# Attention and MLP block on one core: another unit order, with column-tiled products in three runs a unit instead of four

## What is computed

```python
tp = (silu(time_emb) @ Wt + bt)[:, None, :]          # six modulation vectors
h = layernorm(x, g1, be1) * (1 + scale_msa) + shift_msa
q, k, v = split(h @ Wqkv + bqkv)                     # 16 heads of 32
attn = softmax(einsum('blhd,bmhd->bhlm', q, k) * scale)
x = x + gate_msa * (einsum('bhlm,bmhd->blhd', attn, v) @ Wproj + bproj)
h = layernorm(x, g2, be2) * (1 + scale_mlp) + shift_mlp
x = x + gate_mlp * (gelu(h @ W1 + b1) @ W2 + b2)
# then RMSNorm, scale and shift with quantized conditioning weights
```

## Time and profile before

| | us |
|---|---|
| median of 3 runs | 3763.23 (3762.49 to 3764.1) |
| the profiled execution | 3764.97 |
| its span, first to last instruction | 3763.0 |

### The profile page before, as it was taken

How to read it: one execution, slowest core, us unless ns; L and a number is a source line. 1 busy time by engine, 2 the same in 40 slices (tenths; PEclk the granted TensorE clock), 3 DMA queues, 4 the chain that set the end, 5 groups by cost and what they waited for, 6 DMA issues and landing times.

```text
span 3763.0 us, 49948 instructions
## 1 busy us (share of the span) xinstructions
PE 3715.0 (99%) x18430; PEld 2646.7 (70%) x18430; DVE 2453.7 (65%) x4107; ACT 1821.0 (48%) x3276; POOL 1940.8 (52%) x631
## 2 busy tenths in 40 slices
PE   8899999999999999999999999999999999999998
PEld 6688885555555565656565656888888888888887
DVE  5577668888888888888888883333343443443443
ACT  3222225666666666666666665333333333333333
POOL 1000005999999999999999996322222322222221
PEclk9999999999999999999999999999999999999999
DMA  8677876667776777677767755111111111111110
GB/s 286 231 237 241 254 251 142 147 143 160 169 159 148 162 168 157 150 160 170 159 148 161 170 129 159 45 40 50 45 60 45 37 45 37 45 37 45 37 45 23
DMA packets 219003, 479.38 MB, mean 127 GB/s; under 512 B 22809, under 2 KB 61721, under 8 KB 202633
## 3 DMA queue, kind: packets, MB, share of 16 engines
q1 hardware_dynamic: 200616, 344.08, 32.4%
q0 software_dynamic: 18144, 132.13, 17.1%
HBM read 225.36 MB, written 117.60 MB: 91 GB/s over the span
## 4 chain that ended last, share of the span: by engine, by line
PE 89%; POOL 4%; issue 2%; DVE 2%; DMA 2%; ACT 1%; SPq 0%; POOLq 0%; DVEq 0%; ACTq 0%
PE psum L718 12%; PE psum L1276 11%; PE psum L1290 11%; PE psum L581 10%; PE psum L583 10%; PE psum L582 10%; PE psum L1952 6%; PE psum L1948 6%; PE psum L1950 6%; PE psum L1321 4%; POOL probs_round L1555 4%; PE psum L1304 2%; PE psum L1901 1%; DMA token_stats<-packed 0%; DVE qk_out L1155 0%
## 5 line engine op out<-in xcount | busy, mean ns | idle before, releaser
L1100 DVE TENSOR_REDUCE max_part<-psum 128x1 f32<-128x512 f32 x2048 | 1272.7, 679 | 73.4 <-PE psum L718 72.0
L1555 POOL TENSOR_TENSOR probs_round<-probs_round,probs_round 128x2048 f32<-128x2048 f32 x189 | 884.8, 4682 | 126.3 <-PE psum L1290 109.2
L2117 DVE TENSOR_TENSOR g_parts<-g_full,g_parts 128x512 fp32r<-128x512 f32 x256 | 262.7, 1026 | 802.3 <-ACT g_parts L2006 802.3
L1276 PE MATMUL psum<-q_stack,k_stack 98*128 98x512 f32 x2048 | 774.8, 404 | 0.7 <-ACT probs L1422 0.5
L718 PE MATMUL psum<-k_stack,q_stack 96*128 96x512 f32 x2048 | 763.1, 403 | 0.5
L1422 ACT ACTIVATE probs_round<-psum 128x512 f32<-128x512 f32 x1024 | 542.3, 601 | 337.5 <-PE psum L1276 331.6
L1422 ACT ACTIVATE probs<-psum 128x512 f32<-128x512 f32 x1024 | 546.1, 605 | 225.1 <-PE psum L1276 209.0
L1555 POOL TENSOR_TENSOR probs_round<-probs_round,probs 128x2048 f32<-128x2048 f32 x124 | 570.1, 4598 | 9.7
L2002 ACT ACTIVATE g_full<-psum,cols 128x512 f32<-128x512 f32 x256 | 176.6, 690 | 802.2 <-PE psum L583 801.8
L718 PEld LDWEIGHTS psum<-k_stack,q_stack 96*128 96x128 f32 x2048 | 387.0, 189 | 191.5 <-DVE max_part L1100 113.8
L2213 POOL TENSOR_TENSOR y_out<-y_out,rows 128x512 f32<-128x512 f32 x60 | 77.2, 1286 | 857.3 <-DVE y_out L2152 857.3
(11 more groups left out here) (189 smaller groups left out, 4949.8 us busy)
## 6 DMA issues: line engine op xcount, KB each, us to landing
probs<-probs POOLq DMA_DIRECT2D x126, 1024.0 KB, 7.7
qk_parts<-qk_out SPq DMA_DIRECT2D x128, 512.0 KB, 4.6
k_stack<-qk_parts SPq DMA_DIRECT2D x96, 512.0 KB, 6.8
q_stack<-qk_parts SPq DMA_DIRECT2D x192, 256.0 KB, 5.5
v_rows<-v_out SPq DMA_DIRECT2D x64, 256.0 KB, 4.3
v_group<-v_rows SPq DMA_DIRECT2D x32, 512.0 KB, 9.9
gated_attention<-gated SPq DMA_DIRECT2D x64, 256.0 KB, 4.5
x<-in_x SPq DMA_DIRECT2D x16, 1024.0 KB, 9.4
```

The costliest lines, as they stand in the source:

```text
L1100: dve.reduce_max(max_part[:, n:n + 1], psum[:, TURNS[at.turn][0], :], AX.X).then_inc(dve_smax, 1)
L1276: pe.matmul(psum[:, ST[n % 3], :], k_stack[G % 2][0:ROWS, h, kt * P:(kt + 1) * P], q_stack[u % 3][0:ROWS, h, :], start=True, stop=True).th ...
L1555: pool.tensor_tensor(total[:, :, :], total[:, :, :], probs(u, kt)[:, :, :], ALU.add).then_inc(pool_sum, 1)
```

## The change

Two strings are replaced, and one condition in `pool_add`. The counts of all letters stay as they are.

```diff
-    ORDER = ("sgsmmmssmsmaVlVsmsswmmsmsmmVVmsmssmmsmmsmssVV!s"
-             "msmsmsmsmstrmspDVVmjmsjjjnmsmsjsmsjjsmsmjsmjjjj")
+    ORDER = ("gsmssmmsmwVVmsmmsmssmmalVVs!smsjmssmmsjmsmjssmj"
+             "smsmsjsmmsmsjsmsmjsmjmVVDtVrVpnsmsjmmjsmssmjsmj")
...
-    POOL_ORDER = "-1-3-6A-7B5"
+    POOL_ORDER = "-3A-6-7B15"
...
         def pool_add(pool, u, kt):
             total = probs(u, KT - ROTATING)
-            first = kt == SUMS[0]
+            first = kt == (LAST_SUMS if u == NU - 2 else SUMS)[0]
```

## The result

| | before | after |
|---|---|---|
| median, us | 3762.86 (4 runs) | 3943.93 (3939.74 to 3946.5, 4 runs) |
| span of the profiled execution, us | 3763.0 | 3942.3 |
| mean granted clock of PE | 0.997 | 0.977 |

The ratio is 1.048, with a 95% interval of 1.0469 to 1.0495: slower by 181 us. The forecast was slower by 106 us, 3869.2, with a range that ended at 3924. The direction and the wait were as forecast, the cost of the wait was not.

A forecast was written before the change was run, and what follows sets the result against it. PE was taken as the bound in full units, POOL's chain of sums in early ones. Terms -17.3 + 3 + 6.5 - 1.8 + 106.6 + 9 gave +106 us, a median of 3869.2 us, range 3850 to 3924.

The forecast's parts named there:

- The load term's wait: At the first maximum behind "!" in even units, PE waits 4.1 us for keys and queries; bounds 3.75 and 5.9.
- The load term's price: In 26 even full units each wait costs its 4.1 us: +106.6 us, bounds 97 and 153.
- The early units: Units 2, 4, 6, 8, where POOL's chain bounds: the late load costs 2.2 us each, +9 us.
- One run fewer: Column-tiled runs per unit fall from four to three: -0.33 us in each of 52 full units, -17.3 us.
- "!" among ordinary products: The maxima's transpose, moved from a run's end, costs 0.06 us in 52 units: +3 us, upper bound +12.
- Start and tail: Stage 1's extra maxima delay POOL's first sum, +6.5 us; fewer maxima in unit 62 shorten the tail, -1.8 us.
- POOL's order: GpSimd's reordered sums: the chain from V of tile 4 to D stays as long, 0 us.
- The loads in time: Rival: last part lands within 9.1 us of issue, both load terms vanish; -9.6 us, 3753.6 us; chance 0.05.
- The overlap in full: Rival: GpSimd's DMAs B and A share bandwidth equally with the load, landing 16 us, stall 7 us; 3956 us; chance 0.08.
- DVE as the bound: Rival: DVE's idle time runs out, the 26 odd full units grow 1.2 us; +31, 3900 us; chance 0.08.
- the long run: In VVDVV DVE gets no maximum for some 4.6 us of PE time; its slack covers this, costed at nothing.
- D waiting for POOL inside the run: Rival: D waits inside the long run and the saved 0.33 us returns; +17, 3886 us; chance 0.03.

The follow-up runs named there:

- the kernel with five runs: The kernel before, with its first run of two column-tiled groups split by moving one score between them: 3778.61 us, ratio 1.0044.
- the kernel with cut loads: The changed kernel with key and query loads cut in two by heads, each half with its own semaphore: 3755.39 us, ratio 0.9982 to the kernel before.
- the new sums alone: The kernel before with GpSimd's new order of sums and its changed condition, unit order left as it was: 3983.51 us, ratio 1.059.

## Why the prediction was right and wrong

The sum of the differences, from D's starts: 26 even full units of 33.06 instead of 26.84 us, +162; 26 odd ones, -5.5; the four early even units 32.05 in the mean instead of 26.67 (26.25, and 1.7 us more in the first of them, see below), +21.5; the first D +4.1; the last unit and tail -2.5. Together +179, the difference of the spans.

- **The load term's wait: right, its length partly by luck.** A wait at the first maximum behind "!", 30 times, never in odd units. Its length was forecast as 4.1 us, with bounds 3.75 and 5.9, and measured as 4.10 in the mean of PE's idle times. The forecast added 0.35 us for overlaps to a landing of 12.85 us from two samples. That landing was read short: rows 5 give one number for two issues, and in the first sample the last part went out at 1493.41, not 1493.2, and landed 13.2 us behind the first issue. So its slack was 2.3 us and not 2.7. The mean of all 30 loads before is 13.2, and after it is 13.4: the new place cost some 0.2, and A nothing that the runs can tell. The place of the first maximum was right, 9.3 us behind the issue instead of 9.1.
- **The load term's price: the step that failed.** "PE stands for at least 3.75 us in each", taken as 26 x 4.1 = +106.6, prices a wait by its length alone, and the products behind it at full speed. The runs showed 6.45 us a full unit: 4.25 us of standstill and 2.2 us for the stretch at 0.50 behind it, 57 us in 26 units. The early units had 5.8 us instead of 2.2: their waits were 4.7 to 5.0 us, and at the same 45% their stretches at 0.50, of 5.1 to 5.8 us, cost 2.3 to 2.6. The upper bound of 5.9 came from the load alone, and no case had the clock in it.
- **One run fewer, 0.33 us: right,** by the kernel with five runs (0.33) and by the full units: 26.83 - 0.33 + 0.11 = 26.61 us, and 26.60 in most. "!" among ordinary products cost 0.11 us instead of 0.06.
- **Start and tail: right within their bounds.** +6.5 was forecast for POOL's first sum, and it came 4.2 us later (606.84 against 602.66); the tail's last D stands 18.92 us behind the one before it instead of 20.98, -2.1 against -1.8.
- **POOL's order at 0:** nearly right, worth -5 us.
- **The rivals.** The loads in time: false here, and right to 3 us once the loads were cut. The overlap in full: false, the load landed 0.2 us later and not 3. DVE as the bound: false, odd units take 26.6 us and the kernel with cut loads too, so the long run cost nothing by DVE, as forecast. D waiting for POOL inside the run: false for D in full units.

**What the trace of before could have told.** It has such a fall. Behind a wait of only 1.57 us at the first D, in unit 1, PE runs at 0.50 for 3.4 us, and that unit's D takes 1.91 us instead of 1.07:

```profile
626.85 1.91 PE L1304 MATMUL psum<-probs_round,ones 128*32 128x512 f32 x8 [1.57 <-POOL probs_round L1555]
...
627.00:628.00 1.00, 1.00 (x8) 0.30 (x6) 0.00 (x0) 0.00 (x0) 0.54 (x1) 0.50 0.47 90
```

The next D comes after 27.94 us instead of 26.25, and the 1.7 us more are about half of the slow stretch. Waits of 1.3 us in the units that follow, and of 1.83 us in the tail, leave the clock at 1.00. The rows of the prediction begin at the second D and do not show it. The Trainium skill, page "TensorE: Matmul & The Clock Gate", section "HAM oscillation — how this bites in real kernels", describes bursts of products with DMA waits between them, each burst starting at the lower clock. The trace agrees, with 0.50 behind each of the 30 waits.

## What to carry to other kernels

When a hand-written order moves work that runs ahead, follow every transfer that this work needs: from what releases its issue to its last byte, against the new place of its first reader. Here 2.3 us of slack in the mean were used up by a move that no letter of the string shows. And a wait on TensorE is not priced by its length alone: behind 3.5 to 5.2 us of standstill 3.4 to 6.8 us ran at 1.2 GHz, which cost another 2.2 us in the mean of the full units. Look at the granted clock behind the waits that a kernel already has. Where only the first part of a transfer is needed soon, cut it and give each part its own semaphore.

## What the runs showed of the hardware that was not expected

- The granted clock fell to 0.50 at all 30 waits of 3.5 to 5.2 us (changed kernel), at waits of 2.28 us in the full units with the new sums alone, and at one of 1.57 us in the kernel before. It stayed at 1.00 behind the waits of the same length in that run's units 2 to 9 and behind the 1.83 us of the tail before. So the length of a wait did not decide it alone in these runs.
- The fall came between 1.9 us before the wait's end and 1.2 us behind it, and at the 30 waits the clock was low for 3.4 or 6.8 us.
- 17 or 22 products of constant data in the wait kept the clock at 1.00 there, though they compute nothing that is used.
- A change between ordinary and column-tiled products and back costs 0.33 us, of which 0.20 show as longer steps at the run's ends and 0.13 do not.
- 1.5 MB of keys and 0.75 MB of queries took 13.4 us to land in the mean (12.8 to 14.6), whether or not another 1 MB transfer of GpSimd's queue ran beside their end.
